# Gathers with a bounds check: lanes outside the step's tile get an index beyond the table

## What is computed

```
# layer 0, aggregated over row = src
h    = relu(x[row] @ W1[:d] + x[col] @ W1[d:] + b1)
mask = sigmoid(h @ W2 + b2)
agg  = segment_sum(mask / (segment_sum(mask, row)[row] + 1e-9) * x[col], row)
y    = relu(where(deg > 0, 0.5 * x + 0.5 * agg, x) @ Wl + bl)
# layer 1, aggregated over dst
h    = relu(layernorm(concat[x[src], x[dst], e] @ W1 + b1) * ln_g + ln_b)
agg  = segment_sum((h @ W2 + b2) * sigmoid(e @ gate_w + gate_b), dst)
y    = GRU(agg, x)
```

## Time and profile before

| | us |
|---|---|
| median of 3 runs | 5605.35 |
| lowest, highest | 5527.76, 5609.06 |
| the profiled execution, device time | 5597.95 |
| its span in the trace | 5596.0 |

### The profile page before, as it was taken

The page is one execution under the profiler, slowest core; times in us unless marked ns, Lnnn a source line. Parts: engine busy times, 40 slices in busy tenths (PEclk is TensorE's granted clock), DMA queues, the critical chain, the costliest instruction groups (busy, mean ns, idle before and its releaser), DMA issues. The chain is left out here.

```text
span 5596.0 us, 104798 instructions
## 1 busy us (share of the span) xinstructions
PE 3733.5 (67%) x20835; PEld 3292.8 (59%) x20836; DVE 4007.1 (72%) x15198; ACT 2136.7 (38%) x6206; POOL 3338.0 (60%) x3473
## 2 busy tenths in 40 slices
PE   5911266666566566656698666776767777777797
PEld 3711155565556556555576666766767677677564
DVE  8599566666666666666633788888888888888655
ACT  1211122222222222222233655555555555555323
POOL 0000477777777777777500777777777777777310
PEclk6555577667876766787655899888898888888898
DMA  3200344444444444444322444444444444444201
GB/s 110 60 0 0 102 130 128 130 131 129 128 130 130 130 129 130 130 130 129 103 73 69 106 100 103 100 101 102 101 103 101 104 100 101 102 100 103 52 23 59
DMA packets 609827, 558.60 MB, mean 100 GB/s; under 512 B 372594, under 2 KB 475339, under 8 KB 609384
## 3 DMA queue, kind: packets, MB, share of 16 engines
q0 software_dynamic: 133952, 329.07, 21.8%
q1 hardware_dynamic: 475816, 228.86, 15.6%
HBM read 525.30 MB, written 38.57 MB: 101 GB/s over the span
## 5 line engine op out<-in xcount | busy, mean ns | idle before, releaser
L1429 POOL DMA_INDIRECT crows<-c,cols x1664 | 1664.9, 1001 | 511.0 <-issue 475.0
L906 POOL DMA_INDIRECT bxrows<-bx,cols x1664 | 1609.3, 967 | 508.3 <-issue 506.6
L945 PE MATMUL scattered<-bxrows,hotw 128*128 128x129 f32 x3328 | 730.3, 395 | 598.9 <-DVE hotw L1029 598.3
L945 PEld LDWEIGHTS scattered<-bxrows,hotw 128*128 128x128 f32 x3328 | 643.5, 288 | 677.8 <-DVE acc L1026 651.6
L1485 PE MATMUL scattered<-z,hotw 128*128 128x129 f32 x3328 | 629.7, 365 | 542.1 <-DVE hotw L1603 542.1
L1485 PEld LDWEIGHTS scattered<-z,hotw 128*128 128x128 f32 x3328 | 580.1, 267 | 581.0 <-issue 563.4
L935 PE MATMUL pre<-near,hotT 128*128 x3328 | 614.7, 360 | 202.3 <-DVE h L1005 170.3
L1470 PE MATMUL pre<-w1e,efT 128*128 128x129 f32 x3328 | 683.1, 288 | 71.2 <-DVE h L1573 62.8
L935 PEld LDWEIGHTS pre<-near,hotT 128*128 128x128 f32 x3328 | 568.6, 266 | 256.3 <-issue 256.3
L1582 DVE SCALAR_TENSOR_TENSOR z<-h,rstd,ln_g 128x128 f32<-128x128 f32 x1664 | 574.3, 345 | 157.7 <-issue 157.7
L1026 DVE TENSOR_TENSOR acc<-acc,scattered 128x129 f32 x1664 | 467.2, 281 | 272.2 <-ACT mask L983 269.5
(11 more groups left out here) (230 smaller groups left out, 5273.9 us busy)
## 6 DMA issues: line engine op xcount, KB each, us to landing
spread<-place_rows SPq DMA_DIRECT2D x416, 256.0 KB
ef<-in_edge_attr SPq DMA_DIRECT2D x1664, 32.0 KB
bxrows<-bx,cols POOLq DMA_INDIRECT x1664
crows<-c,cols POOLq DMA_INDIRECT x1664
cols<-columns SPq DMA_DIRECT2D x416, 8.0 KB, 1.9
bx<-in_x SPq DMA_DIRECT2D x1, 6250.0 KB
xs<-in_x SPq DMA_DIRECT2D x48, 128.0 KB
bx<-ab SPq DMA_DIRECT2D x48, 128.0 KB, 1.8
```

What stands on the lines that cost most here:

```text
L906: pool.indirect_dma_start(out=bx[q][:, k, 0:2 * D], out_offset=None, in_=s.bx[:, :], in_offset=bass.IndirectOffsetOnAxis(ap=cols[q][:, 0, ...
L945: last = nc.tensor.matmul(out[:, k // 2, k % 2, 0:W], hotw[v % 2][:, k, :], bx[v][:, k, D:D + W], start=True, stop=True)
L1429: pool.indirect_dma_start(out=crows[q][:, k, 0:D], out_offset=None, in_=s.c[:, :], in_offset=bass.IndirectOffsetOnAxis(ap=cols[q][:, 0, k: ...
```

## The change

Three parts. In `schedule_stage`, four more VectorE instructions for each layer work on `columns[l]`: they make a mask of the places from 0 to 127, turn it into 0 (in the tile) or 16,384 (outside), and add that to the index. In both edge stages the indirect DMA gets `bounds_check=N - 1, oob_is_err=False`: an index over 12,499 is then no error, and its row is to be left alone. And the row buffers are set to zero at the start, by GpSimd, with a wait of GpSimd for these memsets; in `edge_stage0` the semaphore it waits for also counts VectorE's memset of `acc`.

```diff
@@ schedule_stage
-                    sp.wait_ge(made[l], 1 + len(widths))
+                    sp.wait_ge(made[l], 2 + len(widths))
                     sp.dma_start(s.columns[l][:, :, :, :], columns[l][:, :, :, :]).then_inc(stored[l], 16)
...
+                    dve.wait_ge(made[l], 1 + len(widths))
+                    place, index = columns[l].bitcast(F32)[:, :, 1, :], columns[l][:, :, 0, :]
+                    dve.tensor_scalar(low[:, :, :], place, 0.0, None, ALU.is_ge).then_inc(bounded[l], 1)
+                    dve.wait_ge(bounded[l], 1)
+                    dve.scalar_tensor_tensor(low[:, :, :], place, float(P - 1), low[:, :, :], ALU.is_le,
+                                             ALU.mult).then_inc(bounded[l], 1)
+                    dve.wait_ge(bounded[l], 2)
+                    dve.tensor_scalar(beyond[:, :, :], low[:, :, :], -float(LOW + 1), float(LOW + 1), ALU.mult,
+                                      ALU.add).then_inc(bounded[l], 1)
+                    dve.wait_ge(bounded[l], 3)
+                    dve.tensor_tensor(index, index, beyond[:, :, :], ALU.add).then_inc(made[l], 1)
@@ edge_stage0
+                    nc.gpsimd.memset(bx[q][:, :, 0:2 * D], 0.0).then_inc(zeroed, 1)
                     nc.gpsimd.memset(bx[q][:, :, 2 * D:2 * D + 1], 1.0).then_inc(zeroed, 1)
...
                             in_offset=bass.IndirectOffsetOnAxis(ap=cols[q][:, 0, k:k + 1], axis=0),
+                            bounds_check=N - 1, oob_is_err=False,
                         ).then_inc(rows_in[q], 16)
+                pool.wait_ge(zeroed, 2 * R + 1)
@@ edge_stage1
-                    nc.gpsimd.memset(crows[q][:, :, D:W], 0.0).then_inc(zeroed, 1)
+                    nc.gpsimd.memset(crows[q][:, :, :], 0.0).then_inc(zeroed, 1)
...
+                            bounds_check=N - 1, oob_is_err=False,
...
+                pool.wait_ge(zeroed, R + 3)
```

More of the change, by code:

```diff
@@ L667, in schedule_stage @@
         turned_up, evac = s.sem("turned_up"), s.sem("evac")
-        rows_made = sem("rows_made")
+        rows_made, bounded = sem("rows_made"), sem("bounded")
+        low = ctx.enter_context(nc.sbuf_tensor("in_tile", [P, GROUPS, G], F32))
+        beyond = ctx.enter_context(nc.sbuf_tensor("beyond", [P, GROUPS, G], I32))
         widths = [min(512, STEPS - 512 * b) for b in range(-(-STEPS // 512))]
@@ L922, in _ @@
             def _(pe):
-                pe.wait_ge(zeroed, R + 1)
+                pe.wait_ge(zeroed, 2 * R + 1)
                 pe.wait_ge(steps_in, 16)
@@ L952, in _ @@
                 act.wait_ge(w_in, 32)
-                act.wait_ge(zeroed, R + 1)
+                act.wait_ge(zeroed, 2 * R + 1)
                 def steps(g, q, o):
@@ L992, in _ @@
                 dve.wait_ge(steps_in, 16)
-                dve.wait_ge(zeroed, R + 1)
+                dve.wait_ge(zeroed, 2 * R + 1)
                 def steps(g, q, o):
```

## The result

The changed kernel takes 5,694 us in the median of 6 runs (5,677 to 5,749), the kernel before 5,571 us (5,528 to 5,609; the 5,605 of the prediction was the median of its first three). The ratio is 1.026, with a 95% interval of 1.020 to 1.033: longer, and by about the 2% that I called the least that can be told for this kernel. The time lies in the predicted range, but the rival "the check costs time in every gather" came true in kind, at half of its price. The six times before fall into two groups, 5,528 to 5,542 and 5,600 to 5,609 us, and the six after too, 5,677 to 5,697 and 5,746 to 5,749; group against group the change is about 150 and 140 us, and both profiled executions are of the upper groups.

A forecast was written before the change was run, and what follows sets the result against it. The prediction took POOL, issuing gathers without a pause, to bound both layers. Its terms, 6.0 + 11.5 + 2.2 = 20 us, were added to 5,605 us for 5,625 us, with a range of 5,420 to 5,960.

The forecast's parts named there:

- the check costs time in every gather: POOL's gathers in both edge stages, duration or gap: all 3,328 pay, 5,958 us at 0.1 us each; chance 0.36.
- likeliest case: Gathers in both edge stages keep their cost, only 20 us are added: 5,625 us; chance 0.48.
- both rivals: Gathers of both layers: left-out lanes save time (5,425 us, chance 0.16), or the check costs time (5,958 us, chance 0.36).
- What binds: Both edge stages: POOL issues 1,664 gathers a layer without a pause, 0.95 + 0.30 us each; the other engines wait.
- Lanes left out save nothing: Gathers in both layers: leaving out 12,992 lanes a layer saves POOL nothing, out of a possible 200 us.
- The check itself: Bound on each of 3,328 gathers: taken as zero, at most 0.2 us each, 666 us; called the weakest step.
- Rival 2: POOL's gathers in both edge stages: the check costs time in all 3,328, deciding from 28 ns, 5,958 us; chance 0.36.
- Register moves 0: GpSimd's moves of the bound ahead of each gather: read as hidden under the gather before, costing nothing.
- Schedule +6.0: Four added VectorE instructions a layer in the schedule: layer 0's fit into a wait, layer 1's add 6.0 us.
- Start of layer 0 +11.5: Before layer 0's first gather: GpSimd's buffer memsets and its wait for the memset of `acc` add 11.5 us.
- Start of layer 1 +2.2: Before layer 1's first gather: four larger POOL memsets of 0.9 us each add 2.2 us.
- The bound of 34 us: Starts of both layers: upper limit of the added sum if POOL's and VectorE's memsets hinder each other, instead of 20 us.

The follow-up runs named there:

- half and quarter gathers: Gathers of 64, then 32 of 128 rows, against the changed kernel without its bound: 5,477 us against 5,536, then 5,417 against 5,542.

## Why the prediction was right in its range and wrong in its likeliest case

- **The time in the range: partly luck.** The range, 5,420 to 5,960 us, took in both rivals. The measured 5,694 lies even in the 5,560 to 5,700 that I gave the likeliest case, and nearer to its 5,625 than to the rival's 5,958. But that case stood on a kernel before of 5,605 us, which over six runs is 5,571. As a ratio it was 1.004, at most 1.017, and 1.026 was measured. The gather rows decide between the cases, not the time.
- **What binds: right.** POOL without a pause; the +126 us between first and last gathers are the +129 us of gather time.
- **Lanes left out save nothing: right.** All 128 out: 0.99 to 1.01 us; half of all out: 1,002 against 998 ns. It was argued from a fixed pass over 128 lanes. The half and quarter gathers bear out the fixed part: at 35 ns for 32 rows, some 830 ns would be left with no row at all (an estimate). They do not bear out a pass of equal cost for each lane. The Trainium skill's section on SWDGE vs HWDGE vs iDMA (DMA: Bandwidth & Descriptors), which has a core computing one descriptor pair per DMA operation, did not turn into a saving for lanes left out. The Trainium skill's section "Anatomy of one DMA — SWDGE (gpsimd) path" on the same page, with descriptor generation small and variable, agrees with 0.7 ns a row for the upper 64 and 1.1 for the next 32.
- **The check itself, taken as 0: the step that failed.** It costs 52 ns a gather, 5.5%, a quarter of my upper bound of 0.2 us. The argument was that a flat time means that a comparison costs next to nothing. A flat time only says that nothing depends on row width or layer; a fixed addition is as flat. The bound of 0.2 us had no footing either: the gather of 1.14 us in the earlier trace rows had no check, and it came after a wait of 344 us for VectorE. What in the gather takes the 52 ns stays open; it is not the register move. Rival 2 had the reach (all gathers) and the point of decision, 28 ns, and left the place open between duration and gap; it is the duration. Its price of 0.1 us was too high. At 3.3 us a nanosecond, 52 ns would be 173 us. The sums rose by only 129, since the means rose by 43 and 34 ns, less than the medians. In layer 1 most of that is in the long gathers: before, 186 were 150 ns or more above the median, 73 us in all, and with the change 49, 25 us (counted in the traces).
- **Register moves 0: right**, by the bound put into a register once: median gather and gap stayed the same.
- **Schedule +6.0: right**, 5.9 from L801 to L814. **Start of layer 0 +11.5:** the first gather came 14.1 us after POOL's first memset began, 2.0 before, so +12.2. **Start of layer 1 +2.2:** 4.45 us against 1.38, so +3.1. Both starts are 0.7 to 0.9 us above their terms, which counted to the end of a memset: from there to the gather it took another 0.8 us. The bound of 34 us for memsets in each other's way was not needed: VectorE's memset of `acc` took 10.59 us both times. The three terms add up to 21 us against 20.
- 20 and 129 us on the profiled 5,598 make 5,747; it was 5,746. So close is chance: the stretches grew by 126, and of the 21.7 us outside them 5.8 came after the last gather, where no term has anything. Before the first gather it was +15.5 against 17.5, between the layers +0.4 against 2.2. The medians of all runs are 123 us apart, since they mix the two groups of times.

## What to carry to other kernels

When one engine issues without a pause, price an option of its instruction at what 1% of that instruction is worth, before asking what the option saves elsewhere: here 9 ns a gather are at most 31 us, and the bytes saved were on engines that had time. Flat durations say that row width doesn't matter, not that an added check is free. A lane left out by a bound did not shorten its gather. Rows not named in the instruction did, but not in proportion, and with 64 rows only one of the two layers got shorter by it. Fewer gathers were not tried.

## What the runs showed of the hardware that I had not expected

- A bound on a 128-row indirect gather: 946 to 998 ns; with its error left on, 1,010 to 1,015. With half the lanes out, 1,002.
- Rows named in the instruction: 128, 64, 32 in 946, 900, 865 ns.
- A queue's packets stay at 133,952 when half of the lanes are left out, and are 107,328 with 64 rows named and with 32.
- The same program took 5,542 to 5,571 us on some chips and 7,086 on another, and there the sign of a 2% change was the other way.
